# A fused LoRA kernel: low-rank A fetched behind x of pair 1, four base blocks ahead, no idle transposes

## The reference

```python
# layer 0: weight[adapter_ids] is (32, 1024, 1024): 16 adapters, one chosen by each sequence
c = einsum('bsi,boi->bso', x, weight[adapter_ids])
logits = c @ W_router.T                       # 8 experts
w = top-2 of softmax(logits), scaled to sum 1 # zero for the other experts
h = einsum('td,erd->ter', c, lora_A)          # rank 16
x = x + c @ W_base.T + b_base + einsum('ter,eor,te->to', h, lora_B, w) * 2
# layer 1: a 64x64 mix by sequence over tokens, then 16 heads of 64
y = einsum('bct,bcd->bdt', x, weights[adapter_ids])
y = per head of the permuted features: gelu(y @ up) @ down, permuted back
x = x + y
```

## Time and profile before

| what | value |
|---|---|
| median of 3 runs | 611.19 us (611.18 to 611.63) |
| profiled execution | 612.55 us, of which span 610.7 us |
| TensorE busy | 593.5 us (97%) |
| VectorE busy | 471.6 us (77%) |
| ScalarE, GpSimd busy | 144.7 us, 128.5 us |
| HBM read, written | 98.09 MB, 8.39 MB |

### The profile page before, as it was taken

The page is one execution under the profiler, slowest core; times in us unless marked ns, Lnnn a source line. Parts: engine busy times, 40 slices in busy tenths (PEclk is TensorE's granted clock), DMA queues, the critical chain, the costliest instruction groups (busy, mean ns, idle before and its releaser), DMA issues.

```text
span 610.7 us, 13500 instructions
## 1 busy us (share of the span) xinstructions
PE 593.5 (97%) x4383; PEld 349.0 (57%) x4384; DVE 471.6 (77%) x1303; ACT 144.7 (24%) x290; POOL 128.5 (21%) x195
## 2 busy tenths in 40 slices
PE   4999999999998999989999999999999999999997
PEld 3344444344433444457767676767676767676773
DVE  3068778878887779698888897879987889887863
ACT  3100000200020002154333523225342325231324
POOL 4010002121111220060022231313131313131312
PEclk9999999999999999999999999999999999999999
DMA  8998998998999987111022222222232223231322
GB/s 264 407 394 315 309 301 293 325 312 301 315 409 402 355 310 254 44 59 39 17 65 90 74 87 71 87 71 91 63 94 68 88 64 97 62 93 60 94 72 86
DMA packets 43427, 106.90 MB, mean 175 GB/s; under 512 B 8450, under 2 KB 17666, under 8 KB 43394
## 3 DMA queue, kind: packets, MB, share of 16 engines
q1 hardware_dynamic: 30914, 76.04, 36.0%
q0 software_dynamic: 6784, 21.51, 10.6%
q10 hardware_dynamic: 5696, 8.95, 4.3%
HBM read 98.09 MB, written 8.39 MB: 174 GB/s over the span
## 4 chain that ended last, share of the span: by engine, by line
PE 86%; DVE 6%; DMA 4%; issue 1%; DVEq 0%; SPq 0%; ACTq 0%; POOL 0%; another core or an unknown queue 0%
PE wide L546 26%; PE bank L653 20%; PE bank L661 10%; PE bank L741 8%; PE wide L724 8%; PE y_wide L577 4%; DVE c_pair L1108 3%; DMA ring<-adapters_dram 3%; PE y_wide L699 3%; PE wide L561 2%; DMA x_in<-x_seq_dram 1%; PE bank L674 1%; PE bank L677 1%; PE bank L673 1%; PE bank L754 1%
## 5 line engine op out<-in xcount | busy, mean ns | idle before, releaser
L546 PE MATMUL wide<-ring,x_in 128*64 128x512 f32 x960 | 209.5, 592 | 1.8 <-DMA ring<-adapters_dram 1.5
L546 PEld LDWEIGHTS wide<-ring,x_in 128*64 128x64 f32 x960 | 73.0, 137 | 126.7 <-issue 126.7
L1306 DVE STREAM_TRANSPOSE x_tok<-xres 32x128 f32<-32x128 f32 x464 | 140.3, 302 | 6.0
L1108 DVE STREAM_TRANSPOSE c_pair<-wide 32x256 f32<-32x256 f32 x240 | 107.1, 446 | 39.5 <-issue 22.1
L955 ACT ACTIVATE act_sb<-wide 128x512 f32<-128x512 f32 x120 | 66.3, 608 | 191.3 <-PE wide L724 191.3
L653 PE MATMUL bank<-c_hi,base_t 128*128 128x512 f32 x384 | 102.3, 390 | 0.0
L430 POOL DMA_INDIRECT xres<-xT_dram,row_in x32 | 34.3, 1073 | 230.1 <-DVE out_sb L1296 226.8
L653 PEld LDWEIGHTS bank<-c_hi,base_t 128*128 128x128 f32 x384 | 71.9, 188 | 15.4
L661 PE MATMUL bank<-c_lo,base_t 128*128 (+1 forms) x256 | 78.0, 390 | 0.0
L468 POOL COPY c_all<-c_pair 128x512 f32 x30 | 19.4, 672 | 213.7 <-DVE c_pair L1108 213.7
L870 ACT ACTIVATE small<-small 128x1 f32<-128x1 f32 x16 | 3.2, 203 | 218.2 <-DVE small L1144 218.2
(11 more groups left out here) (166 smaller groups left out, 605.1 us busy)
## 6 DMA issues: line engine op xcount, KB each, us to landing
ring<-adapters_dram SPq DMA_DIRECT2D x128, 512.0 KB, 5.9
x_in<-x_seq_dram ACTq DMA_DIRECT2D x32, 256.0 KB, 4.9
down_sb<-down_dram SPq DMA_DIRECT2D x32, 128.0 KB
up_raw<-up_dram SPq DMA_DIRECT2D x62, 64.0 KB
ar_sb<-lora_a_router_dram ACTq DMA_DIRECT2D x1, 544.0 KB, 4.3
mix_sb<-mix_dram SPq DMA_DIRECT2D x32, 16.0 KB
xres<-xT_dram,row_in POOLq DMA_INDIRECT x32, 3.4
out_dram<-out_sb,row_out POOLq DMA_INDIRECT x28, 2.9
```

Of the source, the lines that this page charges most:

```text
L546: last = pe.matmul(acc[half][h][z * TOK:(z + 1) * TOK, :], x_in[:, half, z, k, :], ring[:, k, z, h * HALF:(h + 1) * HALF], start=(k == 0), ...
L1108: last = nc.vector.transpose(c_pair[r * SQ:(r + 1) * SQ, :, q * SQ:(q + 1) * SQ], wide[half][q * SQ:(q + 1) * SQ, :, :] .rearrange("p h (k ...
L1306: last = nc.vector.transpose(x1_tok[q * SQ:(q + 1) * SQ, :].rearrange("p (c f) -> p c f", f=P)[:, :, f * SQ:(f + 1) * SQ], xres[f * SQ:(f ...
```

## The change

Low-rank A with the router weights (ar_sb) is no longer issued at the start but behind x of pair 1, on the same queue. SOON becomes 4: block 4 of W_base is a tile now, gathered by GpSimd when x of pair 0 has landed and turned by VectorE (turn_tile(-1)) before the turn of pair 0; the loop over the other three tiles stays (LOOPED = 3) with its counts moved by one. BUSY becomes 0, which takes out the eight transposes. ScalarE copies a column of the identity into th before it waits for the lists. The gathers of lora_b and the bias stand behind pairs 1 to 8. turn_four is cut in two: its first quarter behind the route of the third pair of a round, the other three at the old place. last_seqs on VectorE stands ahead of the turn of pair 14.

```diff
--- before.py
+++ after.py
@@ -56,11 +56,12 @@
 CS = KT // 2
 SPLIT_ORDER = (0, 1, 2, 3, 5, 6, 7)
 C_SLOT = 13
-SOON = 5
-BUSY = 8
+SOON = 4
+LOOPED = KT - SOON - 1
+BUSY = 0
 BATCHED = PAIRS - 4
 TILE_PIECES = (range(0, 6), range(6, 11), range(11, 16))
-GATHERS = range(PAIRS // 4, PAIRS // 4 + KT)
+GATHERS = {j + 1: (j,) for j in range(KT)}
 
 
 def build(nc, xT, x_seq, ids, adapters, w_base, b_base, lora_a_router, lora_b, mix, up, down, perm, out):
@@ -468,16 +469,17 @@
                     pool.tensor_copy(c_all[:, :, bass.ds(seqs[z] * TOK, TOK)], c_pair[:, :, z * TOK:(z + 1) * TOK]) \
                         .then_inc(c_kept, 1)
 
+            pool.wait_ge(x_in_in[0], 32)
+            on_its_own()
+            gather(raw_tile[:, :], w_base, perm_sb[:, SOON:SOON + 1], tile_in)
             pool.wait_ge(order_ok, 1)
             for t in range(PAIRS - 1):
                 keep_pair(t)
-                if t % 4 == 0 and t // 4 < KT - SOON:
-                    j = t // 4 + SOON
-                    if t > 0:
-                        pool.wait_ge(tile_turned, t // 4)
+                if t % 4 == 0 and t // 4 < LOOPED:
+                    j = t // 4 + SOON + 1
+                    pool.wait_ge(tile_turned, t // 4 + 1)
                     gather(raw_tile[:, :], w_base, perm_sb[:, j:j + 1], tile_in)
-                if t in GATHERS:
-                    j = t - GATHERS[0]
+                for j in GATHERS.get(t, ()):
                     gather(b_rows[:, j, :], lora_b, perm_sb[:, j:j + 1], b_in)
                     gather(bias[:, j:j + 1], bias_rows, perm_sb[:, j:j + 1], bias_in)
             pool.wait_ge(base_hi_ok, 5)
@@ -845,7 +847,6 @@
         def _(act):
             act.dma_start(all_ids[:, :], ids.rearrange("(a s) -> a s", a=1).broadcast_to([SEQS, SEQS])) \
                 .then_inc(sort_ids_in, 16)
-            act.dma_start(ar_sb[:, :, :], lora_a_router.rearrange("(k p) e -> p k e", p=P)).then_inc(ar_in, 16)
 
 
             def out_of_acc(t, half):
@@ -894,8 +895,8 @@
 
             def tile_kept(i):
 
-                act.wait_ge(tile_turned, i + 1)
-                nc.scalar.copy(base_rows[:, bass.ds(i + SOON, 1), :, :].rearrange("p a k o -> p (a k o)"), c_tok[:, :]) \
+                act.wait_ge(tile_turned, i + 2)
+                nc.scalar.copy(base_rows[:, bass.ds(i + SOON + 1, 1), :, :].rearrange("p a k o -> p (a k o)"), c_tok[:, :]) \
                     .then_inc(base_turned, 1)
 
             def hw_put(i):
@@ -908,15 +909,19 @@
                             .then_inc(hw_placed, 1)
 
             act.sem_inc(hw_placed, 8)
+            act.wait_ge(ident_ok, 2)
+            nc.scalar.copy(th, ident[:, 0:1])
             act.wait_ge(lists_ok, 1)
             load_x(0, 0)
             for j in range(SOON):
                 base_copied(j)
             load_x(1, 1)
+            act.dma_start(ar_sb[:, :, :], lora_a_router.rearrange("(k p) e -> p k e", p=P)).then_inc(ar_in, 16)
+            tile_kept(-1)
             for half in range(2):
                 next_x(half, half)
                 tanh(half)
-            with act.Fori(0, KT - SOON) as i:
+            with act.Fori(0, LOOPED) as i:
                 for n in range(4):
                     next_x(i * 4 + 2 + n, n % 2)
                     tanh(i * 4 + 2 + n)
@@ -1184,8 +1189,8 @@
 
 
                 if pieces[0] == 0:
-                    dve.wait_ge(tile_in, (i + 1) * 16)
-                    dve.wait_ge(base_turned, i + SOON)
+                    dve.wait_ge(tile_in, (i + 2) * 16)
+                    dve.wait_ge(base_turned, i + SOON + 1)
                 for n in pieces:
                     q, r = n // 4, n % 4
                     last = nc.vector.transpose(
@@ -1194,38 +1199,43 @@
                 if pieces[-1] == 15:
                     last.then_inc(tile_turned, 1)
 
-            def turn_four(i):
-
-
-                dve.wait_ge(hw_ok, i * 4 + 4)
-                dve.wait_ge(hw_placed, i * 8 + 8)
-                for q in range(P // SQ):
+            def turn_four(i, qs):
+
+
+                if qs[0] == 0:
+                    dve.wait_ge(hw_ok, i * 4 + 4)
+                    dve.wait_ge(hw_placed, i * 8 + 8)
+                for q in qs:
                     for r in range(P // SQ):
                         last = nc.vector.transpose(hw_lines[q * SQ:(q + 1) * SQ, :, r * SQ:(r + 1) * SQ],
                                                    hw_four[r * SQ:(r + 1) * SQ, :, q * SQ:(q + 1) * SQ])
-                last.then_inc(hw_turned_ok, 1)
+                if qs[-1] == P // SQ - 1:
+                    last.then_inc(hw_turned_ok, 1)
 
             def pair(t, half):
                 turn_pair(t, half)
                 hw_turned(t - 1)
                 route(t)
 
+            turn_tile(-1, range(0, 16))
             turn_pair(0, 0)
             route(0)
-            with dve.Fori(0, KT - SOON) as i:
+            with dve.Fori(0, LOOPED) as i:
                 for n in range(4):
                     t = i * 4 + 1 + n
                     turn_pair(t, (n + 1) % 2)
                     if n < 3:
                         turn_tile(i, TILE_PIECES[n])
                     else:
-                        turn_four(i)
+                        turn_four(i, range(1, 4))
                     route(t, hw_four[:, (n + 1) % 4, :])
+                    if n == 2:
+                        turn_four(i, range(0, 1))
             pair(PAIRS - 3, 1)
+            seqs = last_seqs(dve)
             turn_pair(PAIRS - 2, 0)
             for j in SPLIT_ORDER[0:3]:
                 base_rest(j)
-            seqs = last_seqs(dve)
             hw_turned(PAIRS - 3)
             route(PAIRS - 2)
             out_of_acc(PAIRS - 1, 1)
```

## The result

The changed kernel takes 620.13 us (618.98 to 620.81, 4 runs) against 611.4 us for the kernel before: ratio 1.0141, interval 1.0123 to 1.0158. It is slower by 8.7 us.

The account below looks back on a forecast made before the run. TensorE, 97% busy, was taken as the bound, with DMA engines nearly full early on. 3.2 (A) + 1.5 (clock) - 0.5 - 0.1 = 4.1 us on 611.19 gave 615.3 us, range 609.6 to 617.6.

Parts of the forecast that it names:

- Low-rank A, 3.2 us: Ahead of pair 1: A's short rows alternate with ring packets, A lands at 35.3, pair 1 starts 3.2 us late.
- The clock after the stall, 1.5 us: At pair 1's start: TensorE's clock falls during the wait for A, costing 1.5 us, bounds 0 to 2.4.
- x 1.7 us sooner: Ahead of the first block: fewer early gathers let x of pair 0 land at 16.5, 1.7 us sooner, bounds 0 and 2.5.
- the second rival: Kernel start: x no sooner, A before 33, small gains against a late VectorE; 610.6 to 611.9 us, chance 0.12.
- The clock in the first gap: Ahead of the first block: a clock fall hidden by the wait for A; with A in time it could cost 1.5.
- The fifth block as a tile at 0, bound 0.7: Before pair 0's router: VectorE turns the late tile in idle time, costing 0, at most 0.7 us.
- turn_four 0.5, gathers 0.1: Near 119 and 189 us: the cut removes a VectorE wait, gaining 0.5; moved gathers ease the ring, gaining 0.1.
- A in time: Ahead of pair 1: seven A rows pass per turn, A lands by 27; 608.9 to 610.4 us, chance 0.20.

Follow-up runs that it names:

- A first: Changed kernel with low-rank A issued at the start again, everything else as changed: 612.22 us, ratio 1.0020.
- A late alone: Kernel before with only low-rank A moved behind x of pair 1: 621.95 us, ratio 1.0174.
- long rows: Changed kernel with A laid out in 128 rows of 4352 bytes instead of 1024 of 544, same place in the queue: 613.37 us, ratio 1.0035.
- loads ahead of the wait: Changed kernel with TensorE's two register loads of landings(1) moved ahead of its wait for A: 616.86 us, ratio 1.0085.
- the tile not late: Changed kernel, A issued at the start, 24 idle transposes, fifth block gathered straight behind the other four, not behind x of pair 0: 611.09 us, ratio 0.9992.
- twenty-four idle transposes: Changed kernel with A issued at the start and BUSY = 24 ahead of the first block: 613.05 us, ratio 1.0020.
- without idle transposes: Kernel before with BUSY = 0, its eight idle transposes taken out, nothing else: 612.1 us, ratio 1.0004.
- small edits alone: Kernel before with only turn_four cut in two and the lora_b and bias gathers behind pairs 1 to 8: 611.32 us, ratio 0.9994.

## Why the prediction was wrong

The direction and the mechanism held; the sum was 4.1 us for 8.7, and the range ended at 617.6. The step that failed is the price of the restart of TensorE after the wait: the register loads (1.76 us) were not in the sum, and the clock was put at 1.5 us and measured 2.9. A smaller error is A's landing. The 0.5 us for turn_four was met by luck. Even with A at 37 and 2.4 us for the clock the prediction's own sum ended at 617.9.

- **Low-rank A, 3.2 us.** Shown by three runs (A first, A late alone, long rows): turns by the packet, 840 to 837. A's rows began to pass near 22.4 us and most were through by 35, almost as forecast (22.5 and 35). But the last packets came after 36, and A landed at 36.85, where I had put 0.3 us between the end and the landing. Why the last ones came so late isn't shown. The bounds of 33.5 and 37 held. Measured term: 36.85 - 32.07 = 4.8 us, or 4.6 us in the chain, which puts the start of pair 1 before at 32.24.
- **Missing from the sum: the register loads, 1.76 us.** The prediction named the blocks queued behind the wait, but not the two loads between the wait and the first of them. TensorE's queue made them at 28.7 us in the kernel before, under the running first block; now they are made after the wait (count, ns min/median/max, first and last start), before and after:

```profile
L532 PEldq TENSOR_LOAD <-order x30: 297/304/484, 28.7 to 250.2; - x30
```

```profile
L534 PEldq TENSOR_LOAD <-order x30: 298/303/487, 37.0 to 257.8; - x30
```

- **The clock after the stall, 1.5 us.** The fall came as forecast, but the sum took less than my own bound, and the bound of 2.4 was itself too low: the level was 0.50 from about 37 to 44, and the five blocks took 2.93 us longer. I had taken the 4.9 us from the first transposes to the rise as the longest; here 5.4 us passed between the first matmul of pair 1 (38.61) and the rise. Nor is the 2.5 us from the end of the work to the fall a fixed delay: it was 4.6 us here, 5.4 with A late alone and 2.1 with the loads ahead of the wait.
- **x 1.7 us sooner.** 1.1 us in the changed kernel, and between 0.5 sooner and 0.2 later in the five others that gather four blocks ahead. x's first packets did come sooner, but three queues then shared the engines, from 10.5 to 13 us:

```profile
q0 software_dynamic: 109, 0.37, 36.2%
q10 hardware_dynamic: 110, 0.22, 31.4%
q1 hardware_dynamic: 67, 0.27, 29.0%
```

  And with the fifth gather back ahead of it (the tile not late) x landed at 17.45. So one gather less is not what sets the landing of x; what does is left open, and where TensorE waited for x the runs lie between 17.2 and 18.6. None of it could show, since A set the start of pair 1. That x would start no sooner was the first half of the second rival, and it nearly came true; its other half, A before 33, did not.
- **The clock in the first gap** fell (0.50 from 17 to 20 us) and was hidden in the wait for A, as the prediction had it. Where nothing hid it, it cost 2.7 us (16.68 against 13.95), more than the 1.5 forecast for that case.
- **The fifth block as a tile at 0, bound 0.7.** Hidden in the changed kernel: VectorE ends pair 0's turn at 33.28 + 7.34 = 40.6, nine us ahead of the router. Where A is in time and the clock stays up it costs 1.6 us (twenty-four idle transposes): x lands later than I took, and so does all behind it.

```profile
26.07 7.18 DVE L1196 STREAM_TRANSPOSE c_tok<-raw_tile 32x256 f32<-32x256 f32 x16 [15.34 <-DMA raw_tile<-w_base_dram,perm_sb]
33.28 7.34 DVE L1113 STREAM_TRANSPOSE c_pair<-wide 32x256 f32<-32x256 f32 x16
```

- **turn_four 0.5, gathers 0.1.** Across the router near 120 the lag falls from 9.3 to 8.6 us. The size is near the forecast, but the cause isn't the cut: in the kernels with A late alone and without idle transposes turn_four is whole, and their routers there (128.62 and 120.32) have no wait for VectorE either, with 0.15 us to spare. The profiled execution of the kernel before had VectorE stand still for 0.76 us ahead of that route, for something that the profile calls only "remote":

```profile
107.91 0.30 DVE L1135 COPY h_l<-y_wide 128x136 f32<-128x136 f32 x1 [0.76 <-remote]
```

  So the wait of the earlier trace rows belonged to that execution, as far as three traces can tell, and no run shows a gain from the cut, only more room for VectorE (0.9 us at the router in the changed kernel). The ring stretch gives 1.0 us instead of 0.1. The two kernels without the small edits gave back 0.1 and 0.2 us over that stretch, the nine with them 0.1 to 1.6; the cause inside it was not taken apart.

The chain closes: 4.6 + 1.8 + 2.9 = 9.3 us at the first router, less 0.7 and 1.0 given back, is 7.6 of span. The medians differ by 1.1 us more. The profiled execution of the kernel before was 1.36 us over its median, and some 0.7 of that may be VectorE's stop; the executions of the changed kernel differ among themselves by as much as 1.8.

Of the rivals, A in time is refuted: seven rows did not pass at a turn. The rule of the Trainium skill ("DMA: Bandwidth & Descriptors", Queues, rings and completion order) that engines go round their queues by the packet agrees with 840 to 837; here each row of ScalarE's queue is a packet of its own (837 packets carry 0.46 MB, 0.55 KB each), and no run shows the 9 to 17 descriptors to a packet that it counts as typical.

## What to carry to other kernels

Where queues take turns by the packet, a transfer of many short rows beside a busy stream lasts as long as its number of rows times a turn; give it long rows, or send it while the others are idle. Put a wait right ahead of the instruction that reads the data (here worth 7.2 us), and register loads ahead of the wait. Price a stall of TensorE with what comes after it, the loads behind the wait and the clock, and when a stall is taken away, look at who was hidden in it. Before a short wait in a trace is put into a sum, look whether it is there in another execution too.

## What the runs showed of the hardware

- 1024 rows of 544 bytes took 20.4 us from issue to landing beside the ring and a raw tile (some 6 us of it behind x of pair 1) and 4.3 us at the start of the kernel without them; 128 rows of 4352 bytes at the same place took 11.7 us. From 25 to 34 us the shares were 840 to 837 packets.
- TensorE's clock fell to 0.50 in stops of 2.16 us (small edits alone), 2.29 (loads ahead of the wait), 2.89 and 5.99 us (changed kernel), and stayed there into dense matmuls: in the changed kernel until about 44 us, over 5 us after they began. Twenty-four transposes that nobody reads (2.78 us) kept it at 1.00 in a gap that cost 2.7 us without them.
- Two register loads and their checks on TensorE's queue take about 1.8 us when nothing runs over them (1.76 us in the changed kernel, 0.04 us left with the loads ahead of the wait).
